# A transformer layer on one core: layer norm folded into the weights, turned queries split out of PSUM, and new instruction lists for every engine

## The reference

```
h  = layernorm(layernorm(x)) * ln_w + ln_b
q, k, v = h @ w_q, h @ w_kv ;  16 heads of 16
q, k = rope(q), rope(k)                       # rotate pairs of columns by the row's angle
t  = 1 + s + s*s/2,  s = (k . q) * 16**-0.5   # Taylor softmax, per head
wv = (t / sum(t)) @ v                         # heads joined, then @ w_o
x1 = x + layernorm(wv @ w_o)
u  = quantise(layernorm(x1))                  # fp6 grid, one scale per 32 columns
out = x1 + layernorm(u @ quantise(w).T + bias)
```

## Time and profile before

| | us |
|---|---|
| median of 3 runs | 649.33 |
| lowest, highest | 647.86, 651.04 |
| span of the profiled execution, first to last instruction | 648.2 |
| DVE busy in it | 605.9 |
| PE busy | 624.1 |
| ACT busy | 569.1 |
| POOL busy | 464.6 |

### The profile page before, as it was taken

How to read it: one execution, slowest core, us unless ns; L and a number is a source line. 1 busy time by engine, 2 the same in 40 slices (tenths; PEclk the granted TensorE clock), 3 DMA queues, 4 the chain that set the end, 5 groups by cost and what they waited for, 6 DMA issues and landing times.

```text
span 648.2 us, 20990 instructions
## 1 busy us (share of the span) xinstructions
PE 624.1 (96%) x6760; PEld 471.8 (73%) x6760; DVE 605.9 (93%) x1424; ACT 569.1 (88%) x1571; POOL 464.6 (72%) x842
## 2 busy tenths in 40 slices
PE   6889999999999999999999999999999999999998
PEld 6676767776777767777776777767767777778887
DVE  5989989999999999999999999999999999996696
ACT  3558899999998999999898999989899999999974
POOL 2675657797778777877787788777777877676364
PEclk9889999999999999999999999999999999999999
DMA  7101121222222232222322222222222212220111
GB/s 245 34 2 35 26 69 31 76 63 54 69 71 81 80 83 72 70 52 69 90 70 84 75 79 50 68 83 71 80 84 79 74 36 53 77 80 28 59 34 50
DMA packets 52362, 43.54 MB, mean 67 GB/s; under 512 B 7200, under 2 KB 48544, under 8 KB 52256
## 3 DMA queue, kind: packets, MB, share of 16 engines
q1 hardware_dynamic: 51440, 41.42, 22.7%
q10 hardware_dynamic: 816, 0.79, 0.4%
HBM read 18.65 MB, written 8.39 MB: 42 GB/s over the span
## 4 chain that ended last, share of the span: by engine, by line
DVE 42%; PE 40%; issue 13%; ACT 2%; POOL 2%; DMA 1%; DVEq 1%; SPq 0%; ACTq 0%; POOLq 0%
DVE kf L540 6%; PE ps_f L689 5%; PE ps_mt L873 5%; DVE xd L1478 4%; DVE kf L1367 4%; PE ps_o L752 4%; DVE z L1340 4%; PE ps_o L755 4%; DVE xs L1452 3%; PE ps_w L644 2%; DVE y L1470 2%; DVE fin L1493 2%; DVE t L1350 2%; DVE fb L1487 2%; PE ps_qk L644 2%
## 5 line engine op out<-in xcount | busy, mean ns | idle before, releaser
L1014 ACT ACTIVATE feat<-ps_f 128x512 f32<-128x512 f32 x256 | 153.1, 604 | 10.9 <-PE ps_f L689 10.2
L689 PE MATMUL ps_f<-qT,selr 128*128 128x512 f32 x320 | 138.0, 436 | 0.6 <-ACT feat L1014 0.6
L540 DVE TENSOR_TENSOR kf<-kf 128x672 f32<-128x672 f32 (+1 forms) x128 | 134.5, 1052 | 2.0
L873 PEld LDWEIGHTS ps_mt<-kf,vp 128*32 128x32 f32 x2048 | 65.5, 109 | 34.1 <-issue 33.3
L1612 POOL TENSOR_TENSOR ve_y<-var_y,epst 128x1 f32<-128x1 f32 x64 | 13.0, 204 | 104.6 <-ACT squares_y L1134 104.5
L873 PE MATMUL ps_mt<-kf,vp 128*32 128x153 f32 x2048 | 78.8, 293 | 0.4 <-ACT rm L1043 0.4
L689 PEld LDWEIGHTS ps_f<-qT,selr 128*128 128x128 f32 x320 | 60.0, 188 | 18.0 <-issue 14.9
L1580 POOL TENSOR_TENSOR hT_l<-hT,hT_h 128x256 fp32r<-128x256 f32 x63 | 56.0, 890 | 23.2 <-ACT hT_h L1079 23.2
L1068 ACT ACTIVATE hT<-ps_tr,small,lnwx 128x128 f32<-128x128 f32 x128 | 51.8, 456 | 20.6 <-PE ps_tr L726 20.5
L752 PE MATMUL ps_o<-feat,main 120*32 120x512 f32 x448 | 59.7, 604 | 0.0
L755 PE MATMUL ps_o<-feat,rm 128*32 128x512 f32 x448 | 58.9, 593 | 0.0
(11 more groups left out here) (190 smaller groups left out, 1955.3 us busy)
## 6 DMA issues: line engine op xcount, KB each, us to landing
xc<-L_attn_x SPq DMA_DIRECT2D x16, 512.0 KB, 4.2
result<-fin SPq DMA_DIRECT2D x64, 128.0 KB, 1.8
xa<-L_attn_x SPq DMA_DIRECT2D x15, 512.0 KB, 4.3
heads_out<-osb SPq DMA_DIRECT2D x224, 32.0 KB, 2.0
shares<-sums SPq DMA_DIRECT2D x112, 64.0 KB
sums<-osb SPq DMA_DIRECT2D x224, 2.0 KB
wkqv<-L_attn_w_kv ACTq DMA_DIRECT2D x2, 256.0 KB, 4.6
xa<-L_attn_x SPq DMA_DIRECT2D x1, 384.0 KB, 5.5
```

Of the source, the lines that this page charges most:

```text
L540: return eng.tensor_tensor(dims(row, F_MAIN, [[FW, heads], [HD, NR - 1], [1, HD]]), dims(row, F_LIN, [[FW, heads], [0, NR - 1], [1, HD]]), ...
L689: pe.matmul(ps_f[i % 2][:, :], selr[:, i], queries, start=True, stop=True).then_inc(sel_done, 1)
L873: mm = pe.matmul(ps_mt[qd // 2][VW * h:VW * (h + 1), (qd % 2) * NF:(qd % 2 + 1) * NF], vp[:, s2, qd * HQ + h], kf[:, s2, qd * HQ + h, 0:NF ...
L1014: act.activation(feat[:, p2, i], ps_f[i % 2][:, :], ACT.Square).then_inc(squared, 1)
```

## The change

- **Layer norm in the weights.** `h` is an affine function of `z`, so ln_w and ln_b go into the weights once. Rows of `z` sum to zero, so the last column is set to one by a memset and its weight row is taken off the others. `z` is then written 255 columns wide. PE multiplies the weights with a matrix `turn` in the setup (`fold_kq`, `fold_v`), and the split of the weights reads PSUM. `copy_h` and `hT` are gone; `high_h` (ACT) and `low_h` (now DVE) read the bank `ps_tr`. The first tile is projected by the same split products as the others.
- **Queries.** `rope_add` adds the keys alone (256 elements, DVE); `add_q` adds the queries on POOL. PE turns them in f32 with two transposes. `high_q` (ACT) and `low_q` (now DVE) write the high and low parts straight into `qT`, each as two instructions over 64 partitions. `copy_q` and the cast of the identity are gone. The row `kf` is 160 per head.
- **Order.** A table `ORDER` gives, for each engine and stage, the place of each tile in the engine's own list: the first ones, a cycle of four that repeats with a pitch, and the last ones. `fill` and `drain` have empty lists. A few waits are added against what the new order could overtake.

```diff
-            def copy_h(t):
-                act.wait_ge(zT_done, t.n)
...
-                for c in range(CH):
-                    ins = act.activation(hT[:, c], ps_tr[:, c * P:(c + 1) * P], ACT.Identity,
-                                         bias=lnb[:, c:c + 1], scale=lnwx[:, c:c + 1])
-                ins.then_inc(hT_copied, 1)
             def high_h(t):
+                act.wait_ge(zT_done, t.n)
...
+                act.activation(hT_h[:, t.two].rearrange("p c n -> p (c n)"), ps_tr[:, 0:D], ACT.Copy).then_inc(hT_high, 1)
+            def low_h(t):                                    # on DVE
+                dve.wait_ge(hT_high, t.n)
+                dve.tensor_tensor(hT_l[:, t.two].rearrange("p c n -> p (c n)"), ps_tr[:, 0:D],
+                                  hT_h[:, t.two].rearrange("p c n -> p (c n)").bitcast(F32), ALU.subtract).then_inc(hT_low, 1)
+        def turned_queries(t, odd, half):
+            return qT[half * HC * HD // 2:(half + 1) * HC * HD // 2, t.par, odd:NQ:2, t.tile * P:(t.tile + 1) * P]
+        def queries_in_bank(odd):
+            return ps_tr[odd * HC * HD // 2:(odd + 1) * HC * HD // 2, 0:D].rearrange("p (c n) -> p c n", c=CH)
             def high_q(t):
+                act.wait_ge(qT_done, t.n)
...
+                for odd in range(2):
+                    ins = act.activation(turned_queries(t, odd, odd), queries_in_bank(odd), ACT.Copy)
+                ins.then_inc(qhi_ready, 1)
+            def low_q(t):                                    # on DVE
+                dve.wait_ge(qhi_ready, t.n)
+                for odd in range(2):
+                    ins = dve.tensor_tensor(turned_queries(t, odd, 1 - odd), queries_in_bank(odd),
+                                            turned_queries(t, odd, odd).bitcast(F32), ALU.subtract)
+                ins.then_inc(qlo_ready, 1)
+            def add_q(t):                                    # on POOL
+                pool.wait_ge(qk_read, 2 * t.n)
+                wait(pool, qT_done, t.n - 2)
+                pool.tensor_tensor(qr[:, t.two], t1[:, D:2 * D], t2[:, D:2 * D], ALU.add).then_inc(q_ready, 1)
             def turn_q(t):
+                pe.wait_ge(q_ready, t.n)
+                turn_bank_is_free()
+                for c in range(CH):
+                    mm = pe.transpose(ps_tr[:, c * P:(c + 1) * P], qr[:, t.two, c * P:(c + 1) * P], ident)
+                mm.then_inc(qT_done, 1)
```

In the setup:

```diff
+            def fold_kq():
...
+                for o in range(CH):
+                    for c in range(CH):
+                        mm = pe.matmul(fold_bank(o)[:, :], turn[:, o, c], wkqv[:, c, 0:2 * D], start=c == 0, stop=c == CH - 1)
+                    mm.then_inc(kq_folded, 1)
```

More of the change, by code:

```diff
@@ L228 @@
-EARLY, LATE = 12, 16
-TAIL = 2
-IDLE_FIRST, IDLE_LAST = 8, 12
-def stage_steps(count):
-    plan = {}
-    for stage, lag in LAG.items():
-        steps = plan.setdefault(stage, {})
-        for tile in range(count):
-            step = tile + lag
-            if tile < EARLY:
-                step += FIRST.get(stage, (0,) * EARLY)[tile]
-            elif tile >= count - LATE:
-                step += FINAL.get(stage, (0,) * LATE)[tile - count + LATE]
-            steps.setdefault(step, []).append(tile)
-    return plan
+TAIL = 2
@@ L248, with places @@
+IDLE = {"fill": (), "drain": ()}
+def places(table, count):
+    first, cycle, last, pitch = table
+    steps = {}
+    for index in range(count):
+        if index < len(first):
+            place = first[index]
+        elif index >= count - len(last):
+            place = last[index - count + len(last)]
+        else:
+            place = cycle[index % len(cycle)] + pitch * (index // len(cycle))
+        steps[place] = index
+    return steps
 FREQS = [0.0, float.fromhex("0x1.be58f4p-4"), float.fromhex("0x1.1bf904p-2"), float.fromhex("0x1.132462p-1"),
@@ L304, in sandwich @@
     TILES = NS * NT
-    plan = stage_steps(TILES)
-    issued = {stage: 0 for stage in plan}
+    BODY = TILES - NT * TAIL
+    assert NT * TAIL == 8
+    counts = {"tile": TILES, "body": BODY, "tail": TILES - BODY, "sequence": NS, "spread": NS - TAIL, "load": NS - 2, "once": 1}
+    plan, issued = {}, {}
+    for engine, (pitch, tables) in ORDER.items():
+        for name, table in tables.items():
+            plan[name] = places(table + (pitch,), counts[RATE.get(name, "tile")])
+            issued[name] = 0
     class Tile:
@@ L351, in wait, with every_step @@
             eng.wait_ge(sem, count)
-    def every_step(step):
-        used = {n for steps in plan.values() for n in steps}
-        for n in range(min(used), max(used) + 1):
+    def every_step(engine, step):
+        last = max(n for name in ORDER[engine][1] for n in plan[name])
+        for n in range(last + 1):
             step(n)
@@ L899, in step @@
             def step(n):
+                idle(n, "fill", fill)
+                idle(n, "drain", drain)
                 setup(n, "warm_up", warm_up)
-                early(n, "fill_a", fill)
+                setup(n, "fold_kq", fold_kq)
+                setup(n, "fold_v", fold_v)
                 each(n, "sum_features", sum_features)
@@ L919, in step @@
                 once(n, "rest_matrix", rest_matrix)
-                each(n, "turn_attention", turn_attention)
+                tail(n, "turn_attention", turn_attention)
                 each(n, "attend", attend)
-                late(n, "drain_a", drain)
-                early(n, "fill_b", fill)
-            every_step(step)
+            every_step("tensor", step)
         @block.scalar
@@ L1162, in step @@
                 each(n, "square_4", square, 4)
-                each(n, "copy_q", copy_q)
                 setup(n, "split_ffn_weight", split_ffn_weight)
@@ L1170, in step @@
                 setup(n, "weight_low", weight_low)
-                each(n, "copy_h", copy_h)
                 setup(n, "sum_wo", sum_wo)
@@ L1533, in step @@
                 each(n, "inverse_scales", inverse_scales)
+                each(n, "low_q", low_q)
+                each(n, "low_h", low_h)
                 each(n, "low_ffn_input", low_ffn_input)
                 each(n, "to_grid", to_grid)
-            every_step(step)
+            every_step("vector", step)
         @block.gpsimd
@@ L1656, in step @@
                 each(n, "products_2", products_2)
-                each(n, "low_q", low_q)
+                each(n, "add_q", add_q)
                 each(n, "add_y", add_y)
```

683 lines of the change are left out of this document (368 added, 315 removed), and 49 rows, old and new, of the table ORDER.

## The result

The changed kernel takes 663.46 us (median of 4 runs, 662.38 to 664.57), the kernel before beside it 650.03. The ratio is 1.0212, 95% interval 1.0195 to 1.0230: slower by 13 us, where I had forecast 643 and faster.

The account below looks back on a forecast made before the run. DVE was taken to set the middle's pace, PE close behind. Span 648.2 - 1 (middle) + 1.5 (setup) + 2 (idle products) - 8 (end order) - 1 (sequence gaps) = 641.7, with 1 around it 643 us; range 626 to 664.

Parts of the forecast that it names:

- Bound of the middle: Steady state, 125 to 565 us: DVE sets the pace at 9.30 us a tile, with PE close behind.
- The parts on DVE: DVE per tile: `low_h` +0.29 us, `low_q` +0.58 and +0.25 lost overlap, `rope_add` -0.26.
- the self-waits: DVE, `block_maxima` to `scales` and `stats_x` to `moments_x`: other work placed between them saves 0.18 us a tile.
- The sum of the middle: DVE's steady tile: 9.30 us becomes 9.28, a draw; over 47 tiles -1 us.
- the sequence's own work: At each fourth tile (inverting sums, rest matrix): the new steady list may close gaps, -1 us in all.
- The stalls behind POOL: DVE's `z`, `xd`, `y` and products, slowed by POOL's SBUF work: 0.86 us a tile, of which 0.7 comes back.
- Rival C: Slower: DVE already full, POOL stalls mostly stay; +0.5 us a tile gives 666, half back 656; chance 0.25.
- The failed step: Fill and drain: 35 us of DVE idle time there; hand-placed order gets under a quarter back, -8 us (0 to -16).
- Ends with clock and setup: Outside the middle: setup +1.5 us, idle products gone +2, fill and drain order -8.
- The signs: Right: tile 9.1 to 9.4 us, `z` near 0.41, `xd` 0.48, end idle under 30; wrong: tile near 9.8.
- Idle products: Fill and drain: without the 88 + 96 matmul records PE may clock lower, +2 us (0 to 8).
- D: Bank `ps_tr` held about 0.7 us longer a tile; losing 0.3 us a tile costs +14, 657 us; chance 0.10.

Follow-up runs that it names:

- a3: Changed kernel with both half-height `low_q` instructions reading and writing partitions 0 to 63, low parts wrong or misplaced: 642.28 us, ratio 0.9897 to the kernel before.
- a2: Changed kernel with `low_q` as one instruction over 128 partitions, low parts wrong or misplaced: 638.31 us, ratio 0.9834 to the kernel before.
- h1: Changed kernel's new stages in the old order on all engines, with the old idle products: 731.06 us, ratio 1.1251 to the kernel before.
- a4: Changed kernel with `low_q` as one 128-partition instruction in the first 16 tiles only, their low parts misplaced: 656.96 us, ratio 1.0129 to the kernel before.
- h3: Changed kernel with everything issued in the first 165 us in the old order: 688.04 us, ratio 1.0580 to the kernel before.
- h2: Changed kernel with everything issued from 565 us on in the old order, without its idle products: 667.73 us, ratio 1.0292 to the kernel before.
- b1: Kernel before without its 88 + 96 idle matmuls of fill and drain: 650.74 us, ratio 1.0017 to the kernel before.
- a1: Changed kernel with some 60 idle matmuls put into the drain: 670.76 us, ratio 1.0329 to the kernel before.
- d1: Changed kernel with the queries going the old way; folded weights, `low_h` on DVE and new order kept: 654.41 us, ratio 1.0070 to the kernel before.
- e1: Changed kernel where, in three tiles of four, one 128-partition `low_q` is made and ScalarE copies place the pieces: 678.20 us, ratio 1.0432 to the kernel before.
- c2: Changed kernel with each query quarter written and turned twice, so one split reads and writes partitions 64 to 127: 677.82 us, ratio 1.0429 to the kernel before.
- c3: Changed kernel where DMAs place low parts in three tiles of four, the others using one 64 x 512 split: 729.54 us, ratio 1.1208 to the kernel before.

## Why the prediction was wrong

- **Bound of the middle, right.** DVE sets the pace of the steady tile, with PE close behind; a3 and a2 show both.
- **The parts on DVE, right.** `low_h`, `low_q` with its side changes, `rope_add`, the self-waits: each within 0.06 us. The sum of the middle was 0.12 us a tile low (idle time, `fin`, `xdT_l`, 672 products), 47 x 0.12 = 5.7 us. Without the 0.18 that the sequence's own work gave back, a term that I had near nothing, it would have been 0.30 low, so its closeness is in part luck. The 0.07 of `fin` is the side change again, at the next read of PSUM.
- **The stalls behind POOL, right.** -0.66 against -0.70. h1 shows that the order did it: without it DVE has 54 us more work. Rival C said that the stalls stay. They went, and the time was C's all the same, so that its number was right for a reason that was wrong.
- **The failed step: "35 us of DVE idle time lie there" and "under a quarter back: -8 us".** I multiplied the DVE terms by the 47 tiles of the middle, put the added work of the other 17 at nothing, and took idle time that goes away for time won. The idle time outside 125 to 565 us did go, from 35.3 to 27.9 us, nearly the 8 that I gave. But in the 17 tiles 12.9 us of work were added, since fewer stalls were there to be given back (`z` took 0.55 us in the mean of the fill of before, 0.68 in its middle), and waiting came back behind the fill, so the idle time of the run stayed at 42 us. a4 shows that the first 16 tiles pay about half of such work or more, 5.4 or 6.5 us of 7.7 by the medians. The order does gain there (h3, h2), but against the old order with the new parts, which is not what stood in the profile of before. Ends with clock and setup: forecast -4.5, measured +9.7; that is 14 of the 20 us of error.
- **The signs, not sharp enough.** The steady tile (9.40 us), `z` and `xd`, and under 30 us of DVE idle time at the ends all came out as "right", and the run was slower. Each half of `low_q` took 0.42 us, where 0.37 was the sign of "right". Of the signs of "wrong" one came, a clock under 0.9 in the drain with PE on the chain, worth an estimated 1.6 us.
- **Idle products, +2 us, not refuted.** b1 gives 1.1 us (-0.5 to 2.6), and the low clock of the drain is some 1.6 by the estimate above. From 20 to 45 us the clock was 1.00 in this execution of after against 0.87, but 0.93 in a1, which has the same fill, so nothing follows from that. As a1 placed them they cost more than the clock gives back.
- **D, the bank `ps_tr`.** In the whole run of after PE's weight loads wait 10.0 us for DVE's `hT_l` and its matmuls 2.0; from 125 to 545 us the matmuls wait 1.3, against the 14 that D would need. Whether these waits cost anything was not tried alone.

## What to carry to other kernels

Count a term of the bounding engine over every tile that it serves, not over the steady ones. Idle time at the ends is not free room: here it took up most of the added work until the first tile was finished, and the waiting came back behind it. Before an engine is relieved or loaded, look at who is next: here PE came to 99% when DVE had lost 0.3 of 9.2 us a tile (a3), and undoing the costliest edit (d1) returned 9 us where DVE's ledger had said 37. When work moves by hand from one in-order list to another (SP, ScalarE), look at what stands behind it there and not at the engine's load alone: ScalarE was busy 83% in e1, and the kernel lost 15 us against after.

## What the runs showed of the hardware

Two VectorE instructions of 64 x 256 that swap the partition halves take 0.42 us each and cost 0.29 us of work a tile more than two that stay in one half (a3). Four instructions start 0.09 to 0.11 us later by the change: both halves, the one behind them, and the first one later that reads PSUM, even with others in between. Staying in the upper half between neighbours that start at partition 0 is a change of side as well (c2). A 64 x 256 and a 128 x 256 subtraction out of PSUM take the same 0.41 us (a3, a2). On GpSimd a 128 x 512 add with repeated reads took 1.38 us (c2) against 0.83 for 128 x 256 (after). A DMA issue held SP's queue for 0.53 to 0.78 us by the median of each kind (c3), not in the order of their sizes: 0.53 for 2 KB, 0.78 for 64 KB of `shares`, 0.58 for 512 KB.
